# Three of eight scan inputs made on ScalarE with tokens on partitions and turned back by TensorE

## What is computed

```python
def _mamba(x, ...):
    ...
    dbc = xs @ x_proj_w.T
    dt = softplus(dbc[..., :DT_RANK] @ dt_proj_w.T + dt_proj_b)
    Bm = dbc[..., DT_RANK:DT_RANK + D_STATE]
    Cm = dbc[..., DT_RANK + D_STATE:]
    dA = exp(dt[..., None] * A)
    dBu = dt[..., None] * Bm[:, :, None, :] * xs[..., None]
    hs = scan of  h = dA * h + dBu  along the tokens
    y = einsum('blds,bls->bld', hs, Cm) + xs * Dvec
    y = y * silu(z)
    return y @ out_proj_w.T
```

## Time and profile before

| | us |
|---|---|
| median of three executions | 646.47 (646.43 to 647.82) |
| the profiled execution, its own time | 647.57 |
| its span in the trace | 645.8 |
| first scan starts | 306.70 |
| last scan starts | 514.8 |
| VectorE busy in the stretch from 306 to 519 | 202.57 of 213 |
| GpSimd busy there | 184.12 |
| TensorE busy there | 166.53 |
| ScalarE busy there | 88.75 |

### The profile page before, as it was taken

One profiled execution on the slowest core, in us unless ns is written; L12 is line 12 of the kernel. 1 busy time (PEld: TensorE's weight loads), 2 busy tenths in 40 slices (PEclk: granted clock), 3 DMA queues, 4 the chain that ended last, 5 costly groups with the idle time before them and its releaser, 6 DMA issues.

```text
span 645.8 us, 6879 instructions
## 1 busy us (share of the span) xinstructions
PE 468.8 (73%) x2535; PEld 291.7 (45%) x2535; DVE 535.7 (83%) x836; ACT 242.6 (38%) x297; POOL 344.8 (53%) x197
## 2 busy tenths in 40 slices
PE   2896989987993998977777876598787888722200
PEld 2255878876982894422222322244433454512200
DVE  4999996997499343388989999999999977787897
ACT  1442413515132136778434344434444405621120
POOL 5153161456063000144699899979989817777303
PEclk9796578987797699988688899989999996855555
DMA  6410000000000001130365775546655401111100
GB/s 195 112 38 1 1 1 3 2 10 1 1 1 8 2 9 46 57 106 33 131 191 172 219 212 211 174 159 244 207 191 183 148 10 10 9 8 8 5 1 32
DMA packets 29587, 50.85 MB, mean 79 GB/s; under 512 B 16144, under 2 KB 18480, under 8 KB 29232
## 3 DMA queue, kind: packets, MB, share of 16 engines
q1 hardware_dynamic: 27760, 49.82, 24.3%
q0 software_dynamic: 1792, 0.58, 1.7%
HBM read 48.62 MB, written 1.77 MB: 78 GB/s over the span
## 4 chain that ended last, share of the span: by engine, by line
DVE 49%; PE 23%; POOL 14%; issue 6%; ACT 6%; DMA 2%; DVEq 0%; SPq 0%; POOLq 0%; ACTq 0%
DVE arena L1582 15%; POOL arena L605 9%; PE ps L676 7%; DVE ps L1572 6%; POOL arena L559 4%; PE ps L845 3%; DVE arena L1358 3%; PE ps L698 3%; DVE arena L1373 2%; PE ps L724 2%; DVE arena L1404 1%; PE ps L661 1%; PE ps L782 1%; POOL arena L552 1%; DVE arena L1356 1%
## 5 line engine op out<-in xcount | busy, mean ns | idle before, releaser
L1582 DVE TENSOR_TENSOR_SCAN arena<-arena,ps 128x1024 f32<-128x1024 f32 x64 | 144.8, 2280 | 10.2 <-POOL arena L559 2.8
L845 PE MATMUL ps<-arena,ident 128*128 128x512 f32 x256 | 130.2, 633 | 20.9 <-POOL arena L559 20.9
L534 POOL TENSOR_TENSOR arena<-arena 128x1536 f32<-128x1536 f32 (+2 forms) x16 | 65.6, 4106 | 111.0 <-DVE arena L1262 60.0
L559 POOL TENSOR_TENSOR arena<-arena 128x1024 f32<-128x1024 f32 x48 | 112.4, 2353 | 23.0 <-PE ps L845 11.9
L1110 ACT ACTIVATE arena<-arena,neg_a 128x1020 f32<-128x1020 f32 x64 | 73.1, 1145 | 120.2 <-DVE arena L1582 116.1
L676 PE MATMUL ps<-arena 128*128 128x64 f32 x576 | 81.0, 311 | 12.5 <-DVE x_tok L1290 12.5
L676 PEld LDWEIGHTS ps<-arena 128*128 128x128 f32 x576 | 80.2, 227 | 12.9 <-issue 12.9
L845 PEld LDWEIGHTS ps<-arena,ident 128*128 128x128 f32 x256 | 49.8, 201 | 71.3 <-issue 36.8
L605 POOL DMA_INDIRECT arena<-node_rows,src_idx x56 | 56.1, 1003 | 31.2 <-issue 16.8
L1572 DVE TENSOR_TENSOR ps<-arena,ps 128x1024 f32<-128x1024 f32 x48 | 58.0, 1208 | 0.3 <-PE ps L835 0.2
L1017 ACT ACTIVATE arena<-ps 128x768 f32<-128x768 f32 x48 | 37.2, 808 | 48.5 <-PE ps L724 48.5
(11 more groups left out here) (344 smaller groups left out, 744.2 us busy)
## 6 DMA issues: line engine op xcount, KB each, us to landing
arena<-state_rows SPq DMA_DIRECT2D x64, 512.0 KB, 4.3
cs<-state_rows SPq DMA_DIRECT2D x16, 512.0 KB, 4.3
arena<-dram_edges SPq DMA_DIRECT2D x2, 1024.0 KB, 8.7
arena<-dram_x SPq DMA_DIRECT2D x2, 512.0 KB, 5.0
arena<-node_rows,src_idx POOLq DMA_INDIRECT x56, 2.9
x_tok<-dram_x SPq DMA_DIRECT2D x1, 512.0 KB, 11.0
res_scratch<-x_tok SPq DMA_DIRECT2D x4, 128.0 KB, 2.0
arena<-res_scratch SPq DMA_DIRECT2D x1, 512.0 KB, 3.3
```

What stands on the lines that cost most here:

```text
L534: g.tensor_tensor(s_buf[i % 2][:, kk], wy[:, i, kk].unsqueeze(3).to_broadcast([P, nk, HEIGHT, WIDTH]), wx[:, i, kk].unsqueeze(2).to_broadc ...
L559: g.tensor_tensor(gg[n % 2], hh[n % 2], cs[n % GROUP], ALU.mult).then_inc(s["g_ready"], 1)
L845: m = pe.matmul(ps[:, 4 + q, :], ident[:], gg[n % 2][:, 512 * q:512 * q + 512], start=False, stop=True, skip_group_check=True)
L1582: v.tensor_tensor_scan(o, x0, x1, 0.0, ALU.mult, ALU.add).then_inc(s["scan_ready"], 1)
```

## The change

Of eight states, the even ones go as before (`rows` on TensorE, multiply on VectorE); state 7 goes the way of GpSimd (`own_b`, now one in eight); and states 1, 3 and 5 go a new way, for which u is kept a second time with tokens on the partitions (`u_tok`) and B as columns (`b_col`):

- `with_b` on ScalarE: eight copies of 128x128, each scaled by one column of B, into `ub` (two buffers). It stands in ScalarE's stream behind the Exp of state n-2.
- `turn_back` on TensorE: eight transposes of 128x128 into PSUM banks 6 and 7. It waits for `ub` and for scan n-2.
- `turn_u` and `u_copy`: for each block, eight transposes of u into banks 2 and 3 and a ScalarE copy of 1024 columns to `u_tok`; ahead of the loop, and at states 8, 21 and 25.
- `b_columns` and a ScalarE copy of 256 columns: 16 matmuls that make B with tokens on partitions, for each direction; ahead of the loop in place of the 12 passes of `stream`, and at state 8. ScalarE's first Exp stands behind the copies of block 0.

The core of the diff:

```diff
+TURN_U_AT = (DS // 2, DS + DS // 4 + 1, DS + DS // 2 + 1)
+TURN = 8
+TURNED = TURN // 2 - 1
+def turned(n):
+    return n // TURN * TURNED + n % TURN // 2
...
-                n = GROUP * grp + GROUP - 1
+                n = TURN * grp + TURN - 1
                 sp.dma_start(bx, row_of(n, n % DS)).then_inc(s["bx_in"], 16)
...
-                if n % GROUP == 0:
-                    b_row(n // GROUP)
+                if n % TURN == 0:
+                    b_row(n // TURN)
...
                 with_c(n)
-                if n % GROUP == GROUP - 1:
-                    own_b(n // GROUP + 1)
+                if n % TURN == TURN - 1:
+                    own_b(n // TURN + 1)
...
+            def b_columns(d, bank):
+                for t in range(NT):
+                    m = pe.matmul(ps[:, bank, DS * t:DS * t + DS], xs[d][:, P * t:P * t + P], xp_w[d][:, 0:DS], start=True, stop=True)
+                m.then_inc(s["bt_psum"], 1)
+            def turn_u(blk):
+                d, c0 = blk // 2, (blk % 2) * HALF
+                pe.wait_ge(s["uu_ready"], d + 1)
+                for q in range(HALF // P):
+                    m = pe.transpose(ps[:, 2 + q // 4, P * (q % 4):P * (q % 4) + P], uu[d][:, c0 + P * q:c0 + P * q + P], ident[:])
+                m.then_inc(s["ut_psum"], 1)
+            def turn_back(n):
+                a = turned(n)
+                pe.wait_ge(s["ub_ready"], a + 1)
+                pe.wait_ge(s["scan_ready"], n + 1)
+                for q in range(HALF // P):
+                    m = pe.transpose(ps[:, 6 + q // 4, P * (q % 4):P * (q % 4) + P], ub[a % 2][:, P * q:P * q + P], ident[:])
+                m.then_inc(s["ub_put"], 1)
...
             rows(0)
+            pe.wait_ge(s["z_ready"], 2)
+            turn_u(0)
             pe.wait_ge(s["z_ready"], 3)
-            stream(Z_STREAM, 4)
+            b_columns(0, 4)
...
-                if n and n % GROUP < GROUP - 1:
+                if n and n % 2 == 0:
                     rows(n)
-                if n == 1:
+                elif n % TURN < TURN - 1 and n:
+                    turn_back(n)
+                if n == 0:
+                    pe.wait_ge(s["bt_ready"], 1)
                     skip_path(0)
...
                     add_state(n - 3)
+                if n in TURN_U_AT:
+                    b = TURN_U_AT.index(n) + 1
+                    pe.wait_ge(s["ut_ready"], b)
+                    turn_u(b)
+                    if b == 1:
+                        pe.wait_ge(s["ut_ready"], 2)
+                        b_columns(1, 2)
...
+            def u_copy(blk):
+                act.wait_ge(s["ut_psum"], blk + 1)
+                if blk < 2:
+                    act.wait_ge(s["z_psum"], 4)
+                f(u_tok[blk], banks(2, 2), ACT.Copy).then_inc(s["ut_ready"], 1)
+            def with_b(n):
+                blk, a = n // DS, turned(n)
...
+                for q in range(HALF // P):
+                    m = f(ub[a % 2][:, P * q:P * q + P], u_tok[blk][:, P * q:P * q + P], ACT.Copy,
+                          scale=b_col[blk // 2][:, (blk % 2) * (HALF // P) + q, n % DS:n % DS + 1])
+                m.then_inc(s["ub_ready"], 1)
...
+                if n == 0:
+                    u_copy(0)
+                    act.wait_ge(s["bt_psum"], 1)
+                    f(b_col[0][:].rearrange("p t n -> p (t n)"), ps[:, 4, 0:NT * DS], ACT.Copy).then_inc(s["bt_ready"], 1)
                 act.wait_ge(s["scan_ready"], n + 1)
...
-                if n % GROUP == GROUP - 1:
+                if n % TURN == TURN - 1:
+                    act.wait_ge(s["bx_ready"], n // TURN + 1)
                     f(banks(6, 2), bx, ACT.Copy).then_inc(s["bx_put"], 1)
+                if n in TURN_U_AT:
+                    u_copy(TURN_U_AT.index(n) + 1)
+                    if n == TURN_U_AT[0]:
+                        act.wait_ge(s["bt_psum"], 2)
+                        f(b_col[1][:].rearrange("p t n -> p (t n)"), ps[:, 2, 0:NT * DS], ACT.Copy).then_inc(s["bt_ready"], 1)
+                m = 1 if n == 0 else n + 2
+                if m % 2 and m % TURN < TURN - 1 and m < STATES:
+                    with_b(m)
...
-                if n % GROUP < GROUP - 1:
-                    made = grp * (GROUP - 1) + n % GROUP + 1
-                    v.wait_ge(s["b_psum"], made)
+                if e == 0:
+                    v.wait_ge(s["b_psum"], n // 2 + 1)
                     tt(b, uu[d][:, c0:c0 + HALF], b, ALU.mult).then_inc(s["b_made"], 1)
```

More of the change, by code:

```diff
@@ L183, in program @@
         pen = sb("pen", [P, NPO, W])
+        b_col = [sb(f"b_col{d}", [P, NT, DS]) for d in range(2)]
         hist_s = sb("hist_s", [P, LO])
@@ L270, in program @@
         state_rows = ar.mem[C:C + 2 * DS, ar.top - T:ar.top]
+        u_tok = [ar.mem[:, HALF * e:HALF * e + HALF] for e in range(2)]
         ar.top = 0
@@ L337, in program @@
         nb_t = br(ROW * WC_MAX)
+        ub = [br(HALF) for _ in range(2)]
+        u_tok.append(br(HALF))
+        u_tok.append(u_tok[0])
+        assert br.top <= br.words
         res_d = nc.dram_tensor("res_scratch", [T, C], F32).ap()
@@ L548, in own_b @@
             def own_b(grp):
-                d, c0 = grp // (2 * GROUP), grp // GROUP % 2 * HALF
+                n = TURN * grp
+                d, c0 = n // (2 * DS), n // DS % 2 * HALF
                 g.wait_ge(s["bx_in"], 16 * grp + 16)
@@ L887, in _ @@
                     pe.wait_ge(s["bc_ready"], 2)
-                if n and n % GROUP < GROUP - 1:
+                    pe.wait_ge(s["ut_ready"], 4)
+                if n and n % 2 == 0:
                     rows(n)
-                if n == 1:
+                elif n % TURN < TURN - 1 and n:
+                    turn_back(n)
+                if n == 0:
+                    pe.wait_ge(s["bt_ready"], 1)
                     skip_path(0)
@@ L896, in _ @@
                     add_state(n - 3)
+                if n in TURN_U_AT:
[5 more added lines that the diff above has]
+                        b_columns(1, 2)
+                elif n == DS + 4:
+                    pe.wait_ge(s["bt_ready"], 2)
                 if blk == 2 and i >= 4:
@@ L1101, in _ @@
             silu_z(1)
+            def u_copy(blk):
[5 more added lines that the diff above has]
+                blk, a = n // DS, turned(n)
+                if a >= 2:
+                    act.wait_ge(s["ub_put"], a - 1)
+                else:
+                    act.wait_ge(s["dt_ready"], 2)
+                act.wait_ge(s["ut_ready"], blk + 1)
+                act.wait_ge(s["bt_ready"], blk // 2 + 1)
+                for q in range(HALF // P):
+                    m = f(ub[a % 2][:, P * q:P * q + P], u_tok[blk][:, P * q:P * q + P], ACT.Copy,
+                          scale=b_col[blk // 2][:, (blk % 2) * (HALF // P) + q, n % DS:n % DS + 1])
+                m.then_inc(s["ub_ready"], 1)
             act.wait_ge(s["nega_ready"], 4)
@@ L1566, in scan_state @@
             def scan_state(n):
-                d, c0, grp, e = n // (2 * DS), n // DS % 2 * HALF, n // GROUP, n % 2
+                d, c0, e = n // (2 * DS), n // DS % 2 * HALF, n % 2
                 b = banks(6 * e, 2)
-                if n % GROUP < GROUP - 1:
-                    made = grp * (GROUP - 1) + n % GROUP + 1
-                    v.wait_ge(s["b_psum"], made)
+                if e == 0:
+                    v.wait_ge(s["b_psum"], n // 2 + 1)
                     tt(b, uu[d][:, c0:c0 + HALF], b, ALU.mult).then_inc(s["b_made"], 1)
@@ L1574, in scan_state @@
                 v.wait_ge(s["g_ready"], n + 1)
-                if n % GROUP < GROUP - 1:
-                    v.wait_ge(s["b_made"], made)
+                if e == 0:
+                    v.wait_ge(s["b_made"], n // 2 + 1)
+                elif n % TURN < TURN - 1:
+                    v.wait_ge(s["ub_put"], turned(n) + 1)
                 else:
-                    v.wait_ge(s["bx_put"], grp + 1)
+                    v.wait_ge(s["bx_put"], n // TURN + 1)
                 o, x0, x1 = hh[e], da[e], b
```

5 lines of the change are left out of this document (2 added, 3 removed).

## The result

The changed kernel takes **641.77 us** (median of four executions, 640.98 to 643.02) beside 647.14 (646.43 to 648.43) for the kernel before on the same chip: a ratio of 0.9919, 95% interval 0.9898 to 0.9939. It is faster by 5.4 us, where 10.4 were forecast. The profiled execution took 641.78, with a span of 640.0.

What follows compares the result with a forecast made beforehand. VectorE was taken to bound the scan stage; −21.8 + 2.6 + 1.3 + 4.2 + 1.3 + 1.0 + 1.0 = −10.4 us took the profiled 647.57 to 637.2, as a median 636.1 us, range 630 to 644.

Steps and rivals of the forecast that it cites:

- 16 multiplies: Scan stage: VectorE multiplies 32 times instead of 48, each worth 1.36 us of its queue, so −21.8 us.
- start: Ahead of scan 0: transposes of u and columns of B delay it from 306.70 to 309.3, +2.6 us; ends +1.3 and +5.1.
- state 1: Scan 1 waits for its `with_b`, which stands behind the first Exp: +1.3 us, +2.4 at the lower clock.
- state 8: ScalarE waits twice for TensorE between two Exps, so scan 9 comes late: +4.2 us, ends +2.5 and +8.
- state 25: `u_copy` waits for `turn_u`, and `with_b(27)` and Exp(26) stand behind it, so scan 26 is late: +1.3 us.
- small waits: Whole scan stage: GpSimd and TensorE late by a few tenths in places, +1.0 us, ends 0.3 and 3.
- clock: Scan stage: TensorE's lowered clock costs +1.0 us more than before, ends −2 and +3.
- tail: Behind the last scan: nothing changes, and the work of GpSimd, TensorE and VectorE moves up as a whole.
- the beat: Steady scans on VectorE: eight states take 22.9 us instead of 25.6.
- the rival of dear copies: ScalarE's small copies cost 0.5 us each instead of 0.30: about +12 us, so 648 us; chance 0.06.
- TensorE did not become the bound for a whole group of states: Rival: TensorE at 1.2 GHz through states 8 to 15 becomes the bound, 654 us; chance 0.06.
- GpSimd did not set the beat: Rival: GpSimd sets the beat, 72 products making 166 us where VectorE needs 183; within the rest, 0.02.

Runs made afterwards that it cites:

- state 29: The changed kernel with the third transpose of u (for block 3) at state 29 instead of 25: 641.09 us, ratio 0.9889.

## Why the prediction was right and where it failed

The terms of the sum beside what the two traces give, in us:

| step | forecast | measured |
|---|---|---|
| 16 multiplies | −21.8 | −21.9 (a pair 5.72, eight states 22.88 against 2 x 12.81) |
| start | +2.6 | +4.3 (scan 0 at 7.09 behind the memset; 2.83 before) |
| state 1 | +1.3 | +2.3 |
| state 8 | +4.2 | +4.0 |
| state 10, behind the columns | 0 | +1.9 |
| state 25 | +1.3 | +1.3 |
| small waits | +1.0 | +1.5 (0.25 + 0.65 + 0.64 ahead of three scans) |
| clock | +1.0 | −1.8, by difference |
| start of the loop | 0 | −0.8 (303.06 instead of 303.87; chance) |
| tail | 0 | +3.4 |
| sum | −10.4 | −5.8, the spans' difference |

The start of the loop is chance: in two traces of the kernel before, with and without passes in the tail, where nothing ahead of the loop differs, it lies at 303.87 and 302.42. With the clock's term, 2.8 better than taken, it hides 3.6 of the 8.2 us that the other steps together came out worse; so that the sum isn't further off is in part luck.

**Right.** The multiply's worth and the beat held to a tenth. `with_b` takes 2.43 us for eight copies, 2.4 forecast, so the rival of dear copies fell. States 8 and 25 cost what was counted out step by step; running the columns in pieces took the wait at state 8 away, and turning u later took 0.6 of the 1.3 at state 25. The price of state 8 holds where the clock falls just behind the columns; where it fell inside them, in the run with wide passes, the same state cost 5.8 us (344.76 − 336.82 − 2.18) instead of 4.0. TensorE did not become the bound for a whole group of states, and GpSimd did not set the beat.

**Failed: "Nothing behind the last scan changes: the tail … moves up as a whole".** This is the largest single miss, 3.4 us. The work did move up as a whole; its clock did not. Filling the gaps brought 3.3 us back, and one more memset 4.0, so neither the experts' work nor what the change does in the scans keeps the clock low there by itself. That it hangs on where the clock's fall lies against the experts' first passes is argued, not shown: falls at 20.0, 20.2, 20.4 and 23.0 us behind the last pair were followed by a return in the experts, falls at 21.3 (wide passes), 21.5 to 21.6 (changed kernel, two and four memsets), 22.3 (state 29) and 23.2 (three memsets) were not, and 23.0 and 23.2 are nearly one place. The cause of the missing return stays open.

**Failed: the start, "TensorE runs at 1.2 GHz from 301 to 304 before; I let it do so again".** The earlier trace rows show the clock with wide passes of 512 columns. The change removed just these and put passes of 16 columns and transposes there, and the clock stayed at 0.50 until 320.2. Counted from the memset, the term was mis-sized by 1.7 us at scan 0 (in the time of the trace by 0.9, 310.15 instead of 309.3, since the loop began 0.8 earlier) and, for the same reason, by 1.0 at scan 1, whose `turn_back` took 1.97 us instead of 0.9 plus its drain. The prediction's own ends (5.1 and 2.4) cover both. The prediction weighed the rule of the Trainium skill (TensorE: Matmul & The Clock Gate, Part 4), that transposes don't count as work for the clock, beside a rival only. The trace of the changed kernel does not speak against it: while 8 transposes and then 32 passes of 16 columns ran, from 299.1 to 307.2, the clock fell to 0.50, at 299.7, and did not come back. But no run here has transposes alone, and in the run with wide passes the clock fell while matmuls of 16 columns ran.

**Failed: nothing was charged behind state 8.** The price there ended with Exp(9). `add_state(6)` and `rows(10)` stand behind the columns on TensorE's queue and ran at the lower clock; spreading the columns took this wait away.

**Better than taken: the clock in the rest of the stage.** The term had −2 as an end and was taken as +1.0. The lateness of block 0, which the earlier trace rows show as 2.0 us, is gone. So is a second one in block 2: before, VectorE waits there at 425.4 and 427.6, together 1.1 us late, behind a stretch in which TensorE has 0.50 (421 to 423); the changed kernel's clock is 1.00 from 359 to 512. Against that, `gated` costs 0.35 us more each of three times. That the first lateness was the clock's is argued, not shown by a run of its own.

## What to carry to other kernels

When an edit takes wide matmuls out of a stretch and puts transposes or narrow passes in, read every later step of that stretch at the lower clock as well as at the higher one, and give the work that stands behind it on TensorE's queue a price as well. A stage that runs unchanged behind the edit can still change its time through the clock: look for the granted clock in its windows, and, if it hangs on a gap, fill the gap. A way that is worth it in the steady part need not be worth its start-up in the first group: here the first eight states are cheaper the old way.

## What the runs showed of the hardware

- Passes of 128x128 weights and 16 columns, back to back, stayed at 1.2 GHz for 6.85 us, and lost 2.4 GHz while running (at 305.8 and 339.9 us in the run with wide passes first). With ten passes of 512 columns in the same place the clock rose, at 302.4 us.
- The experts of the changed kernel ran at 0.50 from 525 to 566 us, the last 21 us of them with TensorE busy for 20.98 and no return.
- One memset of 0.91 us, with its waits 1.3 us of delay, made a kernel 2.1 us faster; in its trace the clock fell 20.4 us behind the last pair instead of 21.6 and came back in the experts.
